# Five of sixteen subtractions that make the experts' low weight parts move from VectorE to GpSimd

## The reference, cut to what matters

```python
logits = x @ router_w
top_val, top_idx = jax.lax.top_k(logits, K)              # K = 2 of E = 8
probs = zeros.at[arange(T)[:, None], top_idx].set(sigmoid(top_val))
xin = probs.T[:, :, None] * x[None]
gu = jnp.einsum('etd,edf->etf', xin, gate_up_w)          # [8, tokens, 512]
gate, up = jnp.split(gu, 2, axis=-1)
h = silu(gate) * up
expert_out = jnp.einsum('eti,eid->etd', h, down_w)
out = x + shared + expert_out.sum(axis=0)
```

## Time and profile before

| | |
|---|---|
| median of three executions | 1227.11 us (1225.47 to 1230.09) |
| the profiled execution | 1225.63 us |
| its span, first to last instruction | 1223.9 us |
| attention, to about 640 us | 640 us |
| shared network and routing, to 784 us | 144 us |
| between the blocks, and weights' split, to 814.5 us | 30.5 us |
| the 71 tiles, to 1213.2 us | 398.7 us |
| rest of the span | 10.7 us |

### The profile page before, as it was taken

The page is one execution under the profiler, slowest core; times in us unless marked ns, Lnnn a source line. Parts: engine busy times, 40 slices in busy tenths (PEclk is TensorE's granted clock), DMA queues, the critical chain, the costliest instruction groups (busy, mean ns, idle before and its releaser), DMA issues. The chain is left out here.

```text
span 1223.9 us, 21492 instructions
## 1 busy us (share of the span) xinstructions
PE 1145.1 (94%) x5638; PEld 706.4 (58%) x5639; DVE 759.7 (62%) x1257; ACT 509.5 (42%) x936; POOL 780.1 (64%) x521
## 2 busy tenths in 40 slices
PE   6999999999999999999999999539999999999994
PEld 2445545555545555555458999526666666666662
DVE  5677776776777767767764854265555554555553
ACT  2456666666666666656652322151111111111110
POOL 1597887977878878778880077624555554555553
PEclk8899999999999999999989999859999999999998
DMA  6668678677686686775553798324445555667771
GB/s 177 181 166 211 189 183 209 181 198 202 182 208 184 175 218 187 195 195 156 162 177 124 271 366 314 109 69 138 152 153 184 173 183 179 209 199 221 218 237 65
DMA packets 116301, 229.49 MB, mean 188 GB/s; under 512 B 19038, under 2 KB 21854, under 8 KB 116256
## 3 DMA queue, kind: packets, MB, share of 16 engines
q1 hardware_dynamic: 84496, 159.30, 44.6%
q0 software_dynamic: 23632, 54.19, 14.9%
q10 hardware_dynamic: 8128, 15.47, 3.8%
HBM read 149.35 MB, written 97.86 MB: 202 GB/s over the span
## 5 line engine op out<-in xcount | busy, mean ns | idle before, releaser
L1043 DVE TENSOR_REDUCE row_max<-bank 128x1 f32<-128x512 f32 x512 | 342.4, 686 | 153.6 <-PE bank L760 151.3
L929 ACT ACTIVATE probsT<-bank 128x512 f32<-128x512 f32 x512 | 299.8, 597 | 201.3 <-PE bank L772 198.2
L606 POOL TENSOR_TENSOR key_sum<-key_sum,probsT 128x1024 f32<-128x1024 f32 x128 | 302.8, 2397 | 0.0
L760 PE MATMUL bank<-k_stack,q_stack 96*128 96x512 f32 x512 | 278.2, 547 | 8.0 <-DMA q_stack<-q_hi 2.6
L602 POOL TENSOR_TENSOR key_sum<-probsT 128x1024 f32<-128x1024 f32 x64 | 152.2, 2389 | 112.2 <-ACT probsT L929 112.2
L772 PE MATMUL bank<-q_stack,k_stack 99*128 99x512 f32 x512 | 207.6, 406 | 3.5 <-ACT probsT L929 3.4
L760 PEld LDWEIGHTS bank<-k_stack,q_stack 96*128 96x128 f32 x512 | 98.2, 192 | 168.4 <-DVE row_max L1043 128.7
L1516 ACT ACTIVATE gated<-bank,slot_info 128x256 f32<-128x256 f32 x71 | 33.7, 474 | 323.4 <-PE bank L1573 323.4
L1566 PE MATMUL bank<-gate_up_hi,rows_hi 128*128 x284 | 137.2, 483 | 15.0 <-issue 14.2
L1592 PE MATMUL bank<-down_sb,act_hT 128*128 x284 | 140.5, 618 | 8.8 <-issue 5.3
L1413 POOL DMA_INDIRECT out<-partner_rows,slot_info x71 | 72.8, 1026 | 112.7 <-DVE partner_rows L1479 112.0
(11 more groups left out here) (145 smaller groups left out, 1730.5 us busy)
## 6 DMA issues: line engine op xcount, KB each, us to landing
expert_rows_dram<-zero_rows SPq DMA_DIRECT2D x16, 1152.0 KB, 7.2
expert_rows_dram<-rows_out SPq DMA_DIRECT2D x71, 256.0 KB, 3.2
k_stack<-hi_dram SPq DMA_DIRECT2D x60, 256.0 KB, 6.5
q_stack<-hi_dram SPq DMA_DIRECT2D x60, 256.0 KB, 7.2
x_row<-in_x SPq DMA_DIRECT2D x16, 512.0 KB, 3.8
rows_ext_dram<-hid SPq DMA_DIRECT2D x16, 512.0 KB, 5.8
hidT_dram<-hidT SPq DMA_DIRECT2D x16, 512.0 KB, 3.0
tok<-hidT_dram SPq DMA_DIRECT2D x16, 512.0 KB, 8.0
```

What stands on the lines that cost most here:

```text
L606: nc.gpsimd.tensor_tensor(total, total, probs(k), ALU.add).then_inc(added, 1)
L760: nc.tensor.matmul(logit_bank[i % 2][:, :], q_stack[par][g][0:K_LOGIT, h, q * P:(q + 1) * P], k_stack[par][g][0:K_LOGIT, h, :], start=True ...
L929: nc.scalar.activation(probsT[:, j, :], key_bank[j % 2][:, :], ACT.Exp, scale=SCALE).then_inc(probs_ready, 1)
L1043: nc.vector.tensor_reduce(row_max[g][:, i:i + 1], logit_bank[i % 2][:, :], AX.X, ALU.max)\
```

## The change

POOL makes the low parts of five chunks, 2, 4, 7, 9 and 12. They stand in its stream behind the two first gathers and the three memsets, and ahead of the wait for the memsets and of its loop. Each waits for the high part of its chunk. DVE makes the other eleven, in the order as before. Both engines count the same semaphore `weights_lo_ready` up, so PE still waits for sixteen.

```diff
             CHUNKS = E * KT // 2
+            BY_POOL = (2, 4, 7, 9, 12)
...
                 for n in range(PARTNERS):
                     nc.gpsimd.memset(partner_rows[n][:, :], 0.0).then_inc(partner_cleared, 1)
+                for c in BY_POOL:
+                    pool.wait_ge(weights_hi_ready, c + 1)
+                    nc.gpsimd.tensor_tensor(weight_chunk(gate_up_lo, c), weight_chunk(gate_up_raw, c),
+                                            weight_chunk(gate_up_hi, c).bitcast(F32), ALU.subtract).then_inc(weights_lo_ready, 1)
                 pool.wait_ge(partner_cleared, PARTNERS)
...
                 for c in range(CHUNKS):
-                    lower_weights(c)
+                    if c not in BY_POOL:
+                        lower_weights(c)
                 lower_in(0)
```

## The result

| | before | after |
|---|---|---|
| median (of 9 executions each) | 1227.11 us | 1234.01 us (1231.26 to 1234.69) |
| ratio | | 1.0049, 95% interval 1.0035 to 1.0063 |
| the profiled execution, its span | 1225.63, 1223.9 us | 1231.26, 1229.3 us |
| ACT's first rounding | 794.01 us | 793.84 us |
| end of DVE's last subtraction | 813.36 us | 820.13 us |

A forecast was written before the change was run, and what follows sets the result against it. PE bounds the tiles; between the blocks, DVE's last low-part subtraction ends last. With turns on the shared access it ends at 819.11 instead of 813.36 us: 1227.11 + 5.75 = 1232.9 us, range 1230.3 to 1236.9.

The forecast's parts named there:

- rival A: Between the blocks, POOL keeps the port for all five subtractions: +6.4 us, 1233.5 us; chance 0.08.
- the turns: POOL's and DVE's SBUF subtractions alternate, 3.30 us a turn, four turns after POOL's first; chance 0.80.
- What bounds: PE bounds the tiles; the change acts only between the blocks, where DVE's last low-part subtraction ends last.
- DVE's saving and its idle time before chunk 3: DVE does 11 chunks instead of 16, 5.7 us less; chunk 3 waits from 797.38 to 797.9 us.
- POOL's rate: Each of POOL's five 128 x 1024 subtractions takes 2.33 us, like the additions of line 606.
- The exclusion: POOL and DVE instructions with two SBUF inputs can't overlap; a moved chunk takes 2.33 us of the shared resource, not 1.14.
- rival B: No exclusion for these tiles in SBUF: DVE is bound by ACT, -2.5 us, 1224.6 us; chance 0.06.
- The cross-check: Shared resource alone: 11 x 1.14 + 5 x 2.33 = 24.2 us, plus 0.5 lost before chunk 3: +6.4 us.
- PE's start: PE's first tile product comes 1.13 us behind DVE's last subtraction, as before, at 820.24 us.
- The gathers: POOL's gathers queued behind its subtractions move from 798.90 to about 814.9 us; no cost, 7.5 us of cover.
- rival C: POOL's delayed gathers come last, tile 2 arriving 2 us late: +8, 1235 us; C or another cost 0.06.
- The clock: PE's clock rises about 6 us after the tiles' products begin, as before: nothing for the term, 1 us either way.

The follow-up runs named there:

- late: The changed kernel with chunks 4, 6, 8, 10 and 13 on POOL; 25.70 us from ACT's first rounding to first product, +5.22 us against before.
- clear_wait: The changed kernel with POOL's wait for its memsets moved ahead of its subtractions; ratio to before 1.0053, first product +5.80 us against before.
- sem_inc: The changed kernel with a semaphore increment between the wait and each POOL subtraction; 27.41 us to first product, +6.93 us against before.
- own_wait: The changed kernel with each POOL subtraction from the second on waiting for the previous one's end; 26.94 us to first product, +6.46 us against before.
- one: The changed kernel with chunk 2 alone on POOL; 22.76 us to first product, +2.28 us against before.
- gather_front: The changed kernel with the memsets moved behind POOL's subtractions and chunks 1, 2, 3, 9, 12 on POOL; 27.01 us to first product, +6.53 us against before.

## Why the prediction held, and where its steps failed

The forecast was 1232.9 us, within a range of 1230.3 to 1236.9, and +0.47%; measured 1234.01 and +0.49%, on the side of slower and by the ratio just inside of 0.5%, for which the text gave 0.58 (by the medians' quotient, +0.56%, just outside). The sum's picture was wrong in one step, and that the number held is in part luck: rival A's 1233.5 us lies 0.6 us beside the forecast, so a time within the range couldn't tell the turns from their failing.

- What bounds: right. The stretch between the blocks took all of the change; the tiles' 397.2 us lie within 1.5 us of before's.
- DVE's saving and its idle time before chunk 3: right (0.48 us of idle time).
- POOL's rate: right, 2.33 to 2.37 us to fp32r, as the additions had it.
- The exclusion: right, and rival B with it gone. The run that only writes shows what B would have been worth, -2.31 us.
- The turns: this step failed. "POOL's first subtraction starts at about 798.7, waits for that, and ends 2.24 us after it": it started at 798.41, didn't wait, and no turn followed. Rival A, given 0.08, is what happened. A's own number was 0.5 us short, since it also let DVE finish chunk 3 first: nine DVE chunks stood behind POOL's, not eight. POOL's end at 809.96 plus 1.09 plus 8 x 1.14 is 820.17; measured 820.13.
- With the turns brought about by one moved wait, DVE's last subtraction is 5.64 us later than before, for the 5.75 of the sum. So the sum was right for the mechanism that it assumed. What was mis-judged is the condition: all the turns in the earlier trace rows lie in one unbroken run of POOL's instructions, whose first, at 621.73 us, had been idle for 3.93 us and came while DVE was in work. I took the pattern for a rule without asking how POOL had come there. The additions of line 606 also wait for POOL's own sum two back (line 604), which the moved subtractions don't; `late` has turns without that.
- Why the number was near all the same: the total work on the shared access is 24.2 us whoever goes first. The cross-check in the prediction, +6.4, was closer than the turn-by-turn sum.
- PE's start: 1.28 us behind DVE's last subtraction, where the sum had 1.13.
- The gathers: no cost, right. They began at 810.12 us, not 814.9, since POOL was through earlier. PE turned tile 2 at 831.26 us without waiting; rival C didn't occur.
- The clock: nearly right to leave at nothing. From the first product to the second tile's first it is 6.77 us after and 6.97 before, 0.2 us given back.

## What to carry to other kernels

In this case GpSimd's work ran beside VectorE's when GpSimd only wrote or VectorE read PSUM. Where both subtract two SBUF operands, add both engines' durations, here 1.20 us of loss for every chunk of 128 x 1024 moved. If it must be so, a wait on GpSimd's own earlier work in front of its reading instructions kept one early instruction of VectorE from waiting for all of them; placed ahead of the first of them (`clear_wait`) it was worth 1.3 us in the traces, too little to show in the timed runs. And when a preparation ends last, look which of its consumers needs the last part: reordering 12 products, with one small subtraction moved ahead, gave 4.2 us, where another engine's help cost 6 to 7.

## What the runs showed of the hardware

A row of DVE that began 0.64 us ahead of a POOL instruction's can still end a whole duration behind it (1.09 us behind POOL's end, where 0.58 were left), when POOL's was queued directly behind memsets: in the kernel after, in `sem_inc`, `own_wait` and `one`. Either what DVE did in those 0.63 to 0.64 us is done again, or POOL had claimed the access before its row begins. The rows can't tell the two apart.

The Trainium skill has the order of issue decide who blocks, and whoever issues first keep the shared pair for its whole instruction (SBUF — State Buffer, Who interferes with whom); it says the second of VectorE's two-port modes. The turns agree with it. By the starts of the rows, chunk 3 of the kernel after, 797.77 us against POOL's 798.41, doesn't; whether POOL's claim came before its row is open.

Most of POOL's indirect DMAs take longer to issue while DVE subtracts two SBUF operands, also where POOL itself isn't at it: 1.66 to 2.05 us against 0.95. The first partner gather of the loop shows it best, beside DVE's subtractions in the kernel after and at their end in `clear_wait`:

```profile
814.44 2.04 POOL L1406 DMA_INDIRECT partner_rows<-expert_rows_dram,slot_info  x1 [0.30 <-issue]
```
```profile
819.74 1.02 POOL L1406 DMA_INDIRECT partner_rows<-expert_rows_dram,slot_info  x1 [0.30 <-issue]
```

It isn't so for each: the second gather of the stretch took 1.14 us beside DVE's subtractions (the kernel before) and 1.14 us with DVE mostly idle (`gather_front`). The DMAs don't hold DVE up, whose rows stay at 1.21 us beside them.

PE's pause at the same place of all fourteen traces was followed by a fall of the granted clock to 0.50 in three of them. The length of the pause doesn't tell which: the clock fell behind 1.51, 1.60 and 1.83 us, and not behind 1.64, 1.67 and 1.79.
